# In a fused recurrence, Silu by way of a tanh and the inverse deviation as a power on GpSimd

## What is computed

```python
def _ln_t(v, eps=1e-05):
    m = jnp.mean(v, axis=-1, keepdims=True)
    s = jnp.var(v, axis=-1, keepdims=True)
    return (v - m) / jnp.sqrt(s + eps)

x_proj = x @ W_in                      # x = _ln_t(t), 64 -> 256
xs, z = jnp.split(x_proj, 2, axis=-1)
delta, Bv, Cv = xs @ W_delta, xs @ W_B, xs @ W_C
def step(state, inp):
    state = exp(delta * A) * state + (delta * Bv) * xs
    return state, einsum('bdn,bn->bd', state, Cv)
y = ys * jax.nn.silu(z)
t = t + y @ W_out
t = t + _L1_ffn_ref(_ln_t(t), ...)
```

## Time and profile before

| what | value |
|---|---|
| median of 3 runs | 6649.49 us (6648.76 to 6650.87) |
| the profiled execution | 6648.02 us |
| its span, first to last instruction | 6646.2 us |
| mean granted TensorE clock | 0.986 |
| scans in the recurrence | 2048, from 1982.35 us of the span on |
| table loads on ScalarE | 128 |

### The profile page before, as it was taken

How to read it: one execution, slowest core, us unless ns; L and a number is a source line. 1 busy time by engine, 2 the same in 40 slices (tenths; PEclk the granted TensorE clock), 3 DMA queues, 4 the chain that set the end, 5 groups by cost and what they waited for, 6 DMA issues and landing times. The chain is left out here.

```text
span 6646.2 us, 155486 instructions
## 1 busy us (share of the span) xinstructions
PE 6210.8 (93%) x52289; PEld 3976.4 (60%) x52289; DVE 6119.4 (92%) x3746; ACT 4632.3 (70%) x9687; POOL 2438.3 (37%) x6919
## 2 busy tenths in 40 slices
PE   8999989999959999999999999999999999999996
PEld 3677744545526666666666666666666666666654
DVE  7888878888839999999999999999999999999995
ACT  7888858888826666666666666666666666666663
POOL 5555545555522333333333333333333333333221
PEclk9999999999969999999999999999999999999998
DMA  6666666666631121212212121221212212121214
GB/s 143 154 155 154 154 146 154 154 154 154 154 94 45 46 58 37 67 45 50 55 40 64 40 58 48 47 58 37 67 45 50 55 40 64 46 52 46 47 31 127
DMA packets 904175, 538.20 MB, mean 81 GB/s; under 512 B 695565, under 2 KB 813997, under 8 KB 903597
## 3 DMA queue, kind: packets, MB, share of 16 engines
q1 hardware_dynamic: 903597, 531.10, 34.1%
HBM read 142.32 MB, written 107.35 MB: 38 GB/s over the span
## 5 line engine op out<-in xcount | busy, mean ns | idle before, releaser
L1220 DVE TENSOR_TENSOR_SCAN states<-decay,enter_ps 128x1024 f32<-128x1024 f32 x2048 | 4489.0, 2264 | 117.7 <-PE enter_ps L800 66.9
L980 ACT ACTIVATE decay<-rate_ps 128x512 f32<-128x512 f32 (+1 forms) x4096 | 2221.6, 594 | 335.0 <-PE rate_ps L786 150.5
L800 PEld LDWEIGHTS enter_ps<-s_steps,s_tokens 128*128 128x128 bf16 x16384 | 1606.4, 129 | 1332.1 <-DVE states L1220 1010.4
L800 PE MATMUL enter_ps<-s_steps,s_tokens 128*128 128x128 bf16 x16384 | 2141.3, 310 | 225.6 <-DVE states L1220 215.8
L786 PE MATMUL rate_ps<-s_wide,s_decays 128*128 128x256 bf16 x8192 | 1328.9, 283 | 61.5 <-ACT decay L980 53.3
L1144 POOL TENSOR_TENSOR product<-decay,states 128x16 f32<-128x16 f32 x1920 | 465.9, 243 | 2086.2 <-ACT decay L980 2078.9
L247 POOL TENSOR_TENSOR entered<-gates 128x512 f32<-128x512 f32 x512 | 901.1, 1760 | 887.8 <-ACT gates L207 887.8
L987 ACT COPY enter_ps<-at_first 128x16 f32<-128x16 f32 x1920 | 338.5, 176 | 1119.6 <-PE enter_ps L800 1081.6
L830 PE MATMUL y_ps<-states,spread 128*32 128x512 f32 x8192 | 1090.3, 604 | 2.4 <-issue 2.4
L786 PEld LDWEIGHTS rate_ps<-s_wide,s_decays 128*128 128x128 bf16 x8192 | 887.8, 118 | 156.5 <-ACT decay L980 83.2
L165 PE MATMUL pre<-rows,weights_left 128*32 128x512 f32 x8192 | 909.2, 595 | 36.7 <-POOL rows L240 23.8
(11 more groups left out here) (137 smaller groups left out, 2498.7 us busy)
## 6 DMA issues: line engine op xcount, KB each, us to landing
rows<-feat SPq DMA_DIRECT2D x1024, 132.0 KB, 2.4
rows<-feat SPq DMA_DIRECT2D x512, 128.0 KB, 2.4
s_steps<-steps_dram SPq DMA_DIRECT2D x4096, 8.0 KB
rows<-feat SPq DMA_DIRECT2D x512, 127.8 KB, 2.4
s_wide<-rates_dram SPq DMA_DIRECT2D x1024, 32.0 KB, 1.9
s_tokens<-tokens_dram SPq DMA_DIRECT2D x2048, 16.0 KB, 2.1
rates_dram<-parts SPq DMA_DIRECT2D x64, 384.0 KB, 3.3
steps_dram<-parts SPq DMA_DIRECT2D x64, 384.0 KB, 3.4
```

Of the source, the lines that this page charges most:

```text
L800: mm = pe.matmul(out.rearrange("p h l -> p l h"), tokens[s][:, k, :], steps[s][:, k, :, d:d + half], start=True, stop=True)
L980: act.activation(decay[i][:, half, at:], rate_ps[h][:, :, at:], ACT.Exp).then_inc(decay_ready, 1)
L1220: dve.tensor_tensor_scan(out, factor, term, 0.0, ALU.mult, ALU.add).then_inc(scanned, 1)
```

## The change

- In Z, ScalarE takes tanh(z / 2) in place of Silu, at unit 2, and copies z itself to `moved` at unit 3. GpSimd multiplies the two at slot 4 and adds z at slot 5 (`z_scaled`, `z_ready`): z tanh(z/2) + z is twice Silu. The half is put into `place`. TURN's multiply now waits for `z_ready`.
- In VARIANCE and G_VAR, ScalarE only adds eps (Identity). GpSimd raises the result to the power -0.5 by `tensor_tensor` with a tile of -0.5, at slot 3 of VARIANCE's chunk and at slot 5 of G_VAR's. VectorE has no reciprocals left, and `invert` and `invert_gate` are gone.

```diff
@@ TensorE, fill_inverse and fill_gate
-                                           inverse[:, k, c:c + 1].broadcast_to([128, CH]), ident[:, :], start=True, stop=True)
+                                           inverse[:, CHUNKS * k + c:CHUNKS * k + c + 1].broadcast_to([128, CH]), ident[:, :], start=True, stop=True)
...
@@ ScalarE
             def first_part(b, n):
-                if STAGES[n][0] == VARIANCE:
+                kind, c = STAGES[n]
+                if kind == VARIANCE:
                     act.wait_ge(var_ready, SCAN0 + b + 1)
-                    act.activation(std[:, :, :].rearrange("p k c -> p (k c)"), work_ps[:, 0:TILES * CHUNKS], ACT.Sqrt,
-                                   bias=eps[:, :]).then_inc(std_ready, 1)
+                    act.wait_ge(inverse_ready, SCAN0 + b)
+                    act.activation(var[:, :], work_ps[:, 0:TILES * CHUNKS], ACT.Identity, bias=eps[:, :]).then_inc(var_moved, 1)
+                elif kind == Z:
+                    act.wait_ge(filled, stages_to(b, n + 1))
+                    if b >= 2:
+                        act.wait_ge(g_filled, gates_to(b - 2, OUT) + 1)
+                    act.activation(gated[b % 2][:, c, :], work_ps[:, :], ACT.Tanh, scale=0.5)
...
-                elif kind == Z:
-                    if b >= 2:
-                        act.wait_ge(g_filled, gates_to(b - 2, OUT) + 1)
-                    a = act.activation(gated[b % 2][:, c, :], work_ps[:, :], ACT.Silu)
...
                     act.wait_ge(left_ready, splits_to(b, n))
+                    if kind == MEAN:
+                        act.wait_ge(z_ready, SCAN0 + CHUNKS * b)
+                    elif kind == Z:
+                        act.wait_ge(z_ready, SCAN0 + CHUNKS * b + c)
                     a = act.copy(moved[:, :], work_ps[:, :])
...
                 if kind == G_VAR:
-                    a = act.activation(g_std[:, :, :].rearrange("p k c -> p (k c)"), work_ps[:, 0:TILES * CHUNKS], ACT.Sqrt,
-                                       bias=eps[:, :])
+                    act.wait_ge(g_inverse_ready, SCAN0 + b)
+                    a = act.activation(g_var[:, :], work_ps[:, 0:TILES * CHUNKS], ACT.Identity, bias=eps[:, :])
@@ GpSimd
+            pool.memset(power[:, :], -0.5)
             pool.memset(eps[:, :], 1e-5).then_inc(eps_set, 1)
+            pool.wait_ge(eps_set, SCAN0 + 1)
...
+                elif kind == VARIANCE and slot == 3:
+                    pool.wait_ge(var_moved, SCAN0 + b + 1)
+                    pool.tensor_tensor(inverse[:, :], var[:, :], power[:, :], ALU.pow).then_inc(inverse_ready, 1)
+                elif kind == Z and slot == 4:
+                    pool.wait_ge(drained, stages_to(b, n + 1))
+                    pool.tensor_tensor(gated[b % 2][:, c, :], gated[b % 2][:, c, :], moved[:, :], ALU.mult
+                                       ).then_inc(z_scaled, 1)
+                elif kind == Z and slot == 5:
+                    pool.wait_ge(z_scaled, SCAN0 + CHUNKS * b + c + 1)
+                    pool.tensor_tensor(gated[b % 2][:, c, :], gated[b % 2][:, c, :], moved[:, :], ALU.add
+                                       ).then_inc(z_ready, 1)
...
-                    pool.wait_ge(drained, stages_to(b + 1, 0))
+                    pool.wait_ge(z_ready, SCAN0 + CHUNKS * (b + 1))
...
+                elif kind == G_VAR and slot == 5:
+                    pool.wait_ge(g_drained, done)
+                    pool.tensor_tensor(g_inverse[:, :], g_var[:, :], power[:, :], ALU.pow).then_inc(g_inverse_ready, 1)
@@ VectorE
-            def invert_gate(b):
-                dve.wait_ge(g_drained, gates_to(b, G_VAR) + 1)
-                dve.reciprocal(g_inverse[:, :, :], g_std[:, :, :]).then_inc(g_inverse_ready, 1)
-
-            def invert(b):
-                dve.wait_ge(std_ready, SCAN0 + b + 1)
-                dve.reciprocal(inverse[:, :, :], std[:, :, :]).then_inc(inverse_ready, 1)
...
-                p = dve.tensor_copy(place[:, SPAN * a:SPAN * a + SPAN].rearrange("p (j e) -> p j e", e=16), rows[:, :, a, :])
+                p = dve.tensor_scalar(place[:, SPAN * a:SPAN * a + SPAN].rearrange("p (j e) -> p j e", e=16), rows[:, :, a, :],
+                                      0.5, None, ALU.mult)
```

More of the change, by code:

```diff
@@ L419, in build_scan @@
         wtok, by_place = sb("wtok", [INNER, 3, 128]), sb("by_place", [INNER, INNER])
-        eps = sb("eps", [128, 1])
+        eps, power = sb("eps", [128, 1]), sb("power", [128, TILES * CHUNKS])
         px, moved, rest, own = (sb(n, [128, BANK]) for n in ("px", "moved", "rest", "own"))
         centred, square, normed = (sb(n, [128, BANK]) for n in ("centred", "square", "normed"))
-        std, inverse = (sb(n, [128, TILES, CHUNKS]) for n in ("std", "inverse"))
+        var, inverse = (sb(n, [128, TILES * CHUNKS]) for n in ("var_tile", "inverse"))
         xs = sb("xs", [INNER, CHUNKS, BANK])
@@ L433, in build_scan @@
         g_moved, g_centred, g_square, g_normed = (sb(n, [128, BANK]) for n in ("g_moved", "g_centred", "g_square", "g_normed"))
-        g_std, g_inverse = (sb(n, [128, TILES, CHUNKS]) for n in ("g_std", "g_inverse"))
+        g_var, g_inverse = (sb(n, [128, TILES * CHUNKS]) for n in ("g_var", "g_inverse"))
         logits = sb("g_logits", [CHUNKS * EXPERTS, BANK])
         weights_in, eps_set, x_in = sem("weights_in"), sem("eps_set"), sem("x_in")
-        g_filled, g_drained, gated_ready, x2_ready, g_centred_ready, g_square_ready, g_inverse_ready, g_normed_ready = (
-            sem("g_filled"), sem("g_drained"), sem("gated"), sem("x2"), sem("g_centred"), sem("g_square"),
+        g_filled, g_drained, z_ready, gated_ready, x2_ready, g_centred_ready, g_square_ready, g_inverse_ready, g_normed_ready = (
+            sem("g_filled"), sem("g_drained"), sem("z"), sem("gated"), sem("x2"), sem("g_centred"), sem("g_square"),
             sem("g_inverse"), sem("g_normed"))
+        z_scaled = sem("z_scaled")
         residual_in, x2_out, normed_out, logits_out, placed = (
             sem("residual_in"), sem("x2_out"), sem("normed_out"), sem("logits_out"), sem("placed"))
-        var_ready, std_ready, inverse_ready = sem("var"), sem("std"), sem("inverse")
+        var_ready, var_moved, inverse_ready = sem("var"), sem("var_moved"), sem("inverse")
         filled, drained, centred_ready, square_ready, normed_ready = (
@@ L867, in fill_gate @@
                             mm = pe.matmul(work_ps[CH * c:CH * c + CH, 128 * k:128 * k + 128],
-                                           g_inverse[:, k, c:c + 1].broadcast_to([128, CH]), ident[:, :],
+                                           g_inverse[:, CHUNKS * k + c:CHUNKS * k + c + 1].broadcast_to([128, CH]), ident[:, :],
                                            start=True, stop=True)
@@ L1205, in batch @@
                     s = set_of(c)
-                    if not ending and g == 3 and STAGES[c][0] == VARIANCE:
-                        invert(b + 1)
-                    if b and u == (GATE_AT + 4) * GROUPS + 7:
-                        invert_gate(b - 1)
                     if g == 0:
@@ L1224, in _ @@
             for a in range(2):
-                p = dve.tensor_copy(place[:, SPAN * a:SPAN * a + SPAN].rearrange("p (j e) -> p j e", e=16), rows[:, :, a, :])
+                p = dve.tensor_scalar(place[:, SPAN * a:SPAN * a + SPAN].rearrange("p (j e) -> p j e", e=16), rows[:, :, a, :],
+                                      0.5, None, ALU.mult)
             p.then_inc(placed, 1)
-            invert(0)
             for b in range(BATCH):
                 batch(b, b == BATCH - 1)
-            invert_gate(BATCH - 1)
 QUADS = BATCH // GROUP
```

## The result

| what | before | after |
|---|---|---|
| median (lowest to highest), 4 runs each | 6649.12 us (6646.91 to 6650.87) | 6594.81 us (6592.79 to 6595.88) |
| ratio | | 0.9918 (0.9901 to 0.9935) |
| span of the profiled execution | 6646.2 us | 6592.7 us |
| mean granted TensorE clock | 0.986 | 0.985 |
| table loads on ScalarE | 128 | 4 |

The change is worth 54.3 us by the medians. The forecast was 6593, from a gain of 56.8. Of the four loads that are left two are in the convolution (L207), one at the start of the recurrence (L987) and one in the experts (L1484).

What follows compares the result with a forecast made beforehand. VectorE's scans, 2.178 us each, bound the recurrence, with 5.49 us a batch lost waiting for ScalarE. 15 x (2.48 + 0.90 + 0.51) = 58.4 us won less 1.6 lost is 56.8, giving 6593 us; range 6585 to 6630.

Steps and rivals of the forecast that it cites:

- Floor and batch: Recurrence on VectorE: scans can't follow faster than 2.178 us each; a batch falls from 284.27 to about 280.4 us.
- Z, 2.48 us a batch: Both halves of Z: without Silu's table loads their whole scan losses, 2.48 us a batch, go.
- G_VAR, 0.90, and VARIANCE, 0.51 gone and 0.56 left: Norm stages, per batch: G_VAR's 0.90 us goes; VARIANCE wins 0.51 and keeps 0.56 behind TensorE's spreading of the inverse.
- The thin losses: 0.47 us before G_VAR and 0.53 after, spread over the previous batch's gate chunks; not tied to loads, expected to stay.
- The power, 1.0 us: GpSimd's power on 128x8 at VARIANCE and G_VAR: estimated at 1.0 us from 40 passes, with no row showing one.
- 2.3 us hidden: At VARIANCE and G_VAR: a power up to about 2.3 us is hidden; above, every microsecond is lost 30 times.
- GpSimd's multiply and add at nothing: Z's two new GpSimd passes, 5.1 us a batch: costed at nothing, with a cover of 0.2 us a unit.
- Rival 1: A long power delays GpSimd's carry and the scans: 6618 us at 3 us, 6842 at 10; chances 12% and 14%.
- Rival 2: GpSimd's new work stretches VectorE's scans in the recurrence, so 46 us of gain would go: 6639 us; 3%.
- Rival 3: Loads weren't what delayed ScalarE in the recurrence; only the reciprocals' 4.5 us go: 6645 us; 3%.
- A load's price: Table loads in the recurrence: at 2.66 us a switch 319 us, called six times what is lost at the scans.
- Outside the recurrence: Serial powers in the prologue and last gate, each replacing a 0.20 us reciprocal: 2 x (1.0 - 0.2) = 1.6 us lost.

Runs made afterwards that it cites:

- experiments 1 and 2: Changed kernel with Silu back in Z, without tanh, copy and GpSimd's multiply and add: 6632.10 us; kernel before with Tanh in place of Silu: 6612.17 us.
- experiment 3: Changed kernel with Sqrt on ScalarE and the reciprocals on VectorE put back, Z still with the tanh: 6611.63 us.
- experiment 4: Kernel before with Identity in place of both Sqrts, reciprocals kept on VectorE, no power on GpSimd: 6632.88 us.
- experiment 8: Changed kernel with TensorE spreading VARIANCE's inverse at the fourth unit of the chunk, in place of the fifth: 6590.45 us.

## Why the prediction was right

The time, 6594.81, is 1.8 us from the forecast, and it came about by the forecast's way. The sizes of some terms were off, and in part they cancelled. Point by point:

- **Floor and batch.** 280.4 us was forecast, 280.44 is there. The recurrence gave 57.4 of the 58.4 us; the missing 1.0 is 15 times 0.06: 3.83 us a batch instead of 3.89.
- **Z, 2.48 us a batch.** Right, by experiments 1 and 2: 37.3 and 37.9 us for 37.2.
- **G_VAR, 0.90, and VARIANCE, 0.51 gone and 0.56 left.** Right in sum: 0.90 + 0.51 is 1.41, and the norms' part is 1.32 a batch by experiment 3 (1.20 by 4, with the reciprocals left in: they cost 0.12, where I had about 0.2 at VARIANCE alone). The gap that stays is 0.50, 0.61 with the overlap, at the seventh unit, behind the spreading of the inverse (L768 now). That it is TensorE's doing was argued from the earlier trace rows; experiments 4 and 8 show it.
- **The thin losses, 1.00 us a batch, left where they are.** Right: 1.05. Single scans in the chunks of OUT, G_INVERSE and SCORE come 0.24 us late, 0.7 us in all, where TensorE has a gate's fill at unit 3 and a contraction at unit 4. None is there in batch 0, which has no gate beside it. That both meet there is what the trace shows; that this makes the scans late is argued, and moving one wasn't tried.
- **The power, 1.0 us.** Mis-sized: 1.648. The estimate counted 40 passes at 2.5 ns a column; the run has 0.158 us a column, some 63 of such passes. That 40 passes were only 0.65 us short is luck, since no row stood behind their number. What saved the forecast was the bound beside it, 2.3 us hidden. It was worked out at VARIANCE, where 2.55 is measured, and taken over for G_VAR, where 2.32 is. The serial powers then cost 2 x 1.45 = 2.9 instead of 1.6.
- **GpSimd's multiply and add at nothing, with a cover of 0.2 us a unit.** The cost was right and the cover wrong: a third pass of 1.04 us costs nothing at the scans. I had set GpSimd's busy time against the length of one unit. But its carry may end anywhere before ScalarE's copy must start, and that leaves over a microsecond. So the nothing that I put down was right for a reason that the prediction didn't have.
- **Rival 1** was real and not met: 16 columns bring it about. As worked out it was too dear (6618 for 3 us, where 6606 was measured with 2.91), since the excess at VARIANCE falls into a gap that is there anyway. **Rival 2**: the scans keep 2.178 us in batch 0 and 280.44 us a batch with GpSimd's new work and even with a third pass. By the rule of the Trainium skill (GPSIMD Engine Reference, Key points), the engines conflict where VectorE has two inputs in SBUF or runs in one of its 2-port modes. A scan reads one of its two inputs from PSUM and isn't slowed, and in that the trace agrees; for the 2-port modes no run here has a row. **Rival 3** fell with experiments 1 to 4.
- **A load's price.** 37.3 us for 60 loads, four in each of 15 batches, is 0.62 us each, of 1.283 us that each takes. The Trainium skill (ScalarE: Activation LUTs, What ACT_TABLE_LOAD costs) has 2.66 a switch; no run here shows that. Not the load's length but what the slack left of it was the price. The norms' 60 loads cost half as much, 16.8 / 60 = 0.28 us each by experiment 4. At G_VAR the activation between the two loads takes 0.27 us where Silu takes 0.60, and a pair costs 0.90 instead of 1.24, which fits. At VARIANCE part of the delay falls into TensorE's gap. The prediction's sum by the length of a switch, 319 us, is 5.5 times the 58.4 that it gave to loads and reciprocals and 3.9 times all that is lost at the scans, not six times.
- **Outside the recurrence** I had 0.8 for each serial power. The prologue's costs 1.5, and the last gate is 1.1 longer. Two scatters, which the prediction didn't reckon with, work against each other in the profiles: 2.8 us more among the experts, and 1.4 less ahead of the recurrence.

The errors: 1.0 us in the recurrence, 0.7 in the prologue, 0.3 in the last gate, and the two scatters: 56.8 - 1.0 - 0.7 - 0.3 - 2.8 + 1.4 = 53.4, within rounding the 53.5 by which the spans differ.

## What to carry to other kernels

Find the floor of the bound engine from a stretch that has no waits, and take all that is over it as the whole of what can be won: here 5.49 us of 284. Then give each operation on a side engine the time until its reader must start, not the room in its own engine's step, and price an excess only beyond a gap that is there already. A new operation of unknown length can be taken if that time is worked out first; and where a gap stays, look which two jobs of TensorE share a unit and part them, as experiment 8 does for another 4 us by the medians.

## What the runs showed of the hardware

- A power of float32 on GpSimd (`tensor_tensor`, `pow`) took 1.648, 2.280 and 2.910 us on 128x8, 128x12 and 128x16: 0.158 us a column and 0.39 us besides. A multiply of 128x512 took 1.267 us, 0.0025 a column: the power costs some 60 times as much.
- GpSimd's multiply of one tile by itself took 1.039 us where two different tiles took 1.267.
- Identity, Tanh, Exp and Copy stood beside each other in the recurrence with no table load between them.
- The same stretch of the expert phase took 15.4 us at a granted clock of 0.77 and 19.7 us at 0.54. TensorE had been at about 0.78 in the stretch before in both; what makes the difference stays open.
